# Moving the value projection ahead of the query and key projections, with a pause between those two, in a two-layer cross-attention decoder

## The chip, the core and the metric

The kernel runs on one core of one Trainium2 chip. Its time is device microseconds of one execution. The core has five engines that run side by side, each through its own list of instructions in order: PE (matrix products; "PEld" is its loading of weights), DVE (vector engine), ACT (scalar engine), POOL (a second, slower vector engine) and SP (which issues the transfers here). They wait for each other on semaphores. A product lands in PSUM, a small memory that DVE and ACT read and empty.

## What is computed

Two decoder layers, one after the other, on 16 sequences of 256 positions with 128 features. Each layer has self-attention, cross-attention over 1601 context positions, and a mixture of experts (8 experts with the best 2 chosen; layer two has one shared expert more). Cut to the attention of layer one:

```python
Q = (q_in @ wq + bq).reshape(Bq, Sq, H, HD)      # H = 16 heads of HD = 8
Kp = (k_in @ wk + bk).reshape(Bq, Sk, H, HD)
V = (v_in @ wv + bv).reshape(Bq, Sk, H, HD)
scores = jnp.einsum('bqhd,bkhd->bhqk', Q, Kp) / jnp.sqrt(jnp.float32(HD))
scores = jnp.where(mask, scores, -jnp.inf)       # causal, self-attention only
o = jnp.einsum('bhqk,bkhd->bqhd', jax.nn.softmax(scores, axis=-1), V)
...
x = layernorm(x + attn(x, x, x, ...)); x = layernorm(x + attn(x, enc, enc, ...)); x = layernorm(x + moe(x, ...))
```

Layer two uses root-mean-square norms ahead of each part, masks that are given as integers, and SiLU in its experts.

## The kernel before, in words

**Rounds.** The work of one batch entry in one layer is spread over three rounds. Round t (t = -1 to 32) does the cross-attention of item t, the experts of item t-1 and, in its first 62%, the self-attention, keys and values of item t+1. Items 0 to 15 are layer one, 16 to 31 are layer two. Rounds 2 to 14 are alike (called the layer-one rounds here), and so are rounds 18 to 30 (the layer-two rounds). All engines are restarted between rounds 15 and 16.

**Steps and the planner.** A round is built from steps with two-letter kinds. The lists of steps of one round are merged by a planner (`weave`): each list has a beginning and an end within the round (self-attention 0.03 to 0.62), and a step's place in it goes by the running sum of costs (`COST`) and pauses (`LATER`, and explicit `pause` steps). A pause emits no instruction. It takes a share of its list's stretch, so it moves the steps behind it and squeezes the others together. The merged order is the order of instructions on every engine.

The steps that matter here:

- QP: a projection of queries or keys. PE makes four products 128x256 (L585); DVE adds the bias into the one buffer `q_sum` (L791); POOL makes `q_high` (L1011) and then `qs` (queries), `ks` (keys) or `qc` (cross-attention's queries) from it (L1014). The DVE instruction of a QP waits until POOL is through with the `q_sum` of the QP before.
- SV: self-attention's values. PE makes two products 128x144 (L591), DVE adds the bias (L796).
- KC: keys of the context, in two pieces; PE L732, then two DVE instructions, `k_hi` (L865) and `k_lo` (L867).
- VC: values of the context (L738, L876). 
- MC: maxima of cross-attention's scores, PE L684, DVE L808 in layer one and L815 in layer two. NR (L820) gathers them and NC (L636, L805) writes them into the queries.
- SC, with its mask product L662 in layer two: cross-attention's scores (L670) with the exponential on ACT (L971). WV: their sums with the values (L700).
- MS, SS, NS, WS: the same four kinds for self-attention (L605 and L618 with L801; L612 and L624 with L966; L636 with L805; L645 with L968).
- OT, OPT, OPM: the output projection (L714, L720, L725). XT: a transpose of x (L579), copied on ACT (L964).
- RM1, LN1: norm statistics on DVE. MK: a mask turned from integers to bf16, on DVE (L885), in layer two.
- RT, R2, R3: the router, many short DVE instructions.

**The two rings.** QP, SV, MS, NS, MC, NC, OT, OPM, KC, VC, RT, EBM and ES all take the next of two PSUM tiles, d0 and d1, in turn. PE may start one only when DVE has read the step two places before it in this ring. Another ring of three tiles, a0 to a2, holds SC, SS, WS and the transposes, which ACT reads.

```python
before, size = rings[ring], slots[ring]
x.ring, x.slot = len(before), len(before) % size
x.prior = before[-size] if len(before) >= size else None
```

So a step that is put in or taken out of the d ring changes the tile and the predecessor of every d step behind it.

Of the kernel before, what the change touches and what calls it, by code (L numbers as in the profile page):

```python
# [161 lines left out]
class Plan:  # L162
# [48 lines left out]
    def self_attention(self, l, p):  # L211
        out = []
# [4 lines left out]
        out.append(xt)  # L217
        if not l:
            out.append(self.put("x_in", "RS", "xs x_in", l=l, role="s", p=p))
        out.append(self.put("qs", "QP", "xs", l=l, i=0, p=p))  # L220
        out.append(self.put("ks", "QP", "xs", l=l, i=1, p=p))
        out.append(self.put("vs", "SV", "xs", l=l, p=p))
        out += self.pause(5.0)
        for g in range(NG + 1):
            for pair in (2, 0):
# [1125 lines left out]
```

How the kernel before makes its waits and increments, by code:

```python
    def mark(self, instruction):  # L516
        instruction.then_inc(self.sem, 1)
        self.n += 1
# [21 lines left out]
def wait_made(engine, M, x):  # L540
    if x.kind in D_RING:
        engine.wait_ge(M["d_read"], in_ring(x))
    elif x.kind in A_RING:
        engine.wait_ge(M["a_read"], in_ring(x))
    elif x.kind == "LX":
        engine.wait_ge(M["x_loaded"], 16 * nth(x))
    elif x.kind == "LN2":
        engine.wait_ge(M["ln_scaled"], nth(x))
    elif x.kind == "RM2":
        engine.wait_ge(M["rm_done"], nth(x))
    elif x.kind == "RS":
        engine.wait_ge(M["bias_added"], nth(x))
# [2 lines left out]
def wait_empty(pe, M, x):  # L556
    if x.prior:
        pe.wait_ge(M["d_read" if x.kind in D_RING else "a_read"], in_ring(x.prior))
        if x.prior.kind == "EF" and x.prior.l == 1:
            pe.wait_ge(M["silu_done"], x.prior.j + 1)
    return x.slot
# [2 lines left out]
def tensor_program(pe, T, M, order):  # L565
# [12 lines left out]
            for qt in range(QT):  # L578
                last = pe.transpose(tile[:, qt * P:(qt + 1) * P], source[:, qt, :], T["ident"][:])
            last.then_inc(M["a_made"], 1)
        elif x.kind == "QP":
            source = T["xT_c" if x.i == 2 else "xT_s"]
            pe.wait_ge(M["a_read"], in_ring(x.of["xc" if x.i == 2 else "xs"]))
            for g in range(NG):
                last = pe.matmul(tile[:, g * S:(g + 1) * S], T["w_pad"][:, x.l, x.i, g, :], source[:], start=True,
# [1 line left out]
            last.then_inc(M["d_made"], 1)  # L587
        elif x.kind == "SV":
            pe.wait_ge(M["a_read"], in_ring(x.of["xs"]))
            for kt in range(QT):
```

## Time and profile before

| | us |
|---|---|
| median of three runs | 5493.64 |
| lowest and highest | 5491.49 and 5499.58 |
| the profiled execution | 5490.66 |
| its span, first to last instruction | 5489.3 |
| PE busy | 4937.0 (90%) |
| DVE busy | 3496.5 (64%) |
| ACT busy | 2792.3 (51%) |
| POOL busy | 641.3 (12%) |

Times within the trace are microseconds from the first instruction. A busy time is the union of an engine's instructions. In a row of the timeline, the bracket at the end is the time for which the engine sat idle before it, and the instruction that ended this. The granted clock of PE has two levels, 1.2 GHz (0.5) and 2.4 GHz (1.0); a mean over a stretch lies between.

### The profile page before, as it was taken

What the parts mean: (1) busy time and instruction counts of PE and PEld (TensorE: products, weight loads), DVE (VectorE), ACT (ScalarE), POOL (GpSimd) and SP (SyncE); (2) the same over time, 40 slices, a digit from 0 to 9 for tenths busy, and PEclk for the clock granted to TensorE, in tenths of its full rate; (3) what the DMA queues carried; (4) which work ended last, traced back from release to release, by engine and by line L of the source; (5) the groups of instructions that cost most, each with busy time, mean ns of one, the idle gap of its engine ahead of it and who ended that gap; (6) DMA issues with size and microseconds to landing.
All of it is one profiled execution on the core that took longest, in us unless ns stands there. A gap on an engine that the chain in (4) does not pass through costs nothing.

```text
span 5489.3 us, 101033 instructions
## 1 busy us (share of the span) xinstructions
PE 4937.0 (90%) x40898; PEld 2789.8 (51%) x41312; DVE 3496.5 (64%) x6335; ACT 2792.3 (51%) x5505; POOL 641.3 (12%) x660
## 2 busy tenths in 40 slices
PE   5888888888888888889899999999999999999999
PEld 2455555555555555555355544554455544554456
DVE  4666666665666666665566667666666666666664
ACT  1565565666655555665454444444444444444444
POOL 1111111111111111111110001101010101101000
PEclk7799999999999999998899999999999999999999
DMA  2112222222221222222122222222222222222211
GB/s 59 34 45 54 47 43 47 58 54 57 47 55 44 43 47 58 53 67 66 49 73 73 68 62 73 72 64 75 62 72 72 72 64 67 73 70 68 68 47 64
DMA packets 167976, 326.96 MB, mean 60 GB/s; under 512 B 25656, under 2 KB 76624, under 8 KB 167520
## 3 DMA queue, kind: packets, MB, share of 16 engines
q1 hardware_dynamic: 167520, 320.49, 23.6%
q8 instruction: 334, 5.47, 0.4%
q14 instruction: 122, 1.00, 0.1%
HBM read 237.40 MB, written 4.19 MB: 44 GB/s over the span
## 4 chain that ended last, share of the span: by engine, by line
PE 43%; DVE 4%; ACT 2%; issue 1%; POOL 1%; DVEq 0%
PE a L662 7%; PE sums L700 7%; PE a L670 6%; PE d L776 6%; PE a L764 5%; PE d L684 3%; DVE d L815 2%; ACT probs_c L971 1%; PE d L738 1%; PE d L585 1%; PE a L612 1%; PE d L732 1%; PE a L645 1%; PE d L605 1%; PE d L618 1%
## 5 line engine op out<-in xcount | busy, mean ns | idle before, releaser
L971 ACT ACTIVATE probs_c<-a 128x512 f32<-128x512 f32 (+1 forms) x3584 | 1833.9, 563 | 2084.6 <-PE a L670 2082.7
L815 DVE CUSTOM_DVE_ANT_0 d<-d,mcross_q 128x808 f32<-128x808 f32 x1024 | 1023.3, 1012 | 470.9 <-PE d L684 468.0
L808 DVE TENSOR_REDUCE chunk_max<-d 128x2 f32<-128x808 f32 x1024 | 1003.5, 998 | 288.7 <-PE d L684 280.1
L700 PE MATMUL sums<-probs_c,vc 128*32 128x256 f32 x13312 | 1113.6, 408 | 13.0 <-PEq L1238 12.8
L684 PE MATMUL d<-kc,qc 24*128 24x404 f32 x4096 | 1080.3, 433 | 34.0 <-DVE chunk_max L808 11.1
L670 PE MATMUL a<-qc,kc 25*128 25x256 f32 (+1 forms) x6656 | 934.4, 340 | 130.0 <-ACT probs_c L971 98.9
L670 PEld LDWEIGHTS a<-qc,kc 25*128 25x128 f32 (+1 forms) x6656 | 548.1, 187 | 820.4 <-issue 387.4
L776 PE MATMUL d<-w_back,hidden 128*128 128x128 f32 x4352 | 567.3, 285 | 25.8 <-DVE chunk_max L815 25.8
L776 PEld LDWEIGHTS d<-w_back,hidden 128*128 128x128 f32 x4352 | 542.7, 200 | 73.9 <-DVE chunk_max L815 34.7
L764 PE MATMUL a<-xT_e,w_in 128*128 128x256 f32 x2176 | 579.3, 413 | 0.0
L952 DVE SCALAR_TENSOR_TENSOR xe<-d,comb,xe 128x128 f32<-128x128 f32 x544 | 165.8, 347 | 589.6 <-PE d L776 589.6
L684 PEld LDWEIGHTS d<-kc,qc 24*128 24x128 f32 x4096 | 499.9, 192 | 74.1 <-DVE chunk_max L808 35.0
L662 PE MATMUL a<-mcross_k,ident_b 128*128 128x512 bf16 (+1 forms) x1507 | 482.9, 375 | 59.9 <-ACT probs_c L971 26.7
L764 PEld LDWEIGHTS a<-xT_e,w_in 128*128 128x128 f32 x2176 | 419.3, 203 | 94.9 <-issue 33.7
L700 PEld LDWEIGHTS sums<-probs_c,vc 128*32 128x32 f32 x13312 | 275.3, 111 | 357.9 <-issue 201.7
L966 ACT ACTIVATE probs_s<-a 128x512 f32<-128x512 f32 x512 | 277.9, 594 | 263.6 <-PE a L624 263.6
L801 DVE TENSOR_REDUCE nm_s<-d 128x4 f32<-128x1024 f32 x256 | 313.5, 1225 | 120.8 <-PE d L618 120.7
L662 PEld LDWEIGHTS a<-mcross_k,ident_b 128*128 128x128 bf16 (+1 forms) x1792 | 143.8, 99 | 436.9 <-issue 272.6
L944 DVE SCALAR_TENSOR_TENSOR hidden<-hidden,a 128x512 f32<-128x512 f32 x288 | 198.1, 688 | 126.2 <-ACT hidden L994 125.1
L990 ACT ACTIVATE hidden<-a,b_hid 128x256 f32<-128x256 f32 x512 | 208.6, 476 | 90.6 <-PE a L764 87.1
L1043 POOL TENSOR_TENSOR rstd_s<-mean_var_s,halves 128x2 f32<-128x2 f32 x32 | 22.5, 703 | 1931.4 <-DVE mean_var_s L857 1931.4
L994 ACT ACTIVATE hidden<-a 128x512 f32<-128x512 f32 x288 | 172.0, 597 | 97.9 <-PE a L764 96.3
(157 smaller groups left out, 4358.0 us busy)
## 6 DMA issues: line engine op xcount, KB each, us to landing
w_in<-in_experts SPq DMA_DIRECT2D x272, 256.0 KB, 3.1
w_back<-in_experts SPq DMA_DIRECT2D x272, 256.0 KB, 2.9
kc<-k_hi SPq DMA_DIRECT2D x1024, 50.0 KB
ctxT<-in_ctxT SPq DMA_DIRECT2D x32, 800.5 KB, 5.0
kc<-k_lo SPq DMA_DIRECT2D x512, 50.0 KB
mask_words<-in_mcross SPq DMA_DIRECT2D x32, 800.5 KB
mask_words<-in_mcrossT SPq DMA_DIRECT2D x32, 768.0 KB
out_x<-xe SPq DMA_DIRECT2D x32, 128.0 KB, 1.8
```

Of the source, the lines that this page charges most:

```text
L662: pe.matmul(T["a"][y.slot][0:y.kn, 0:n * S], T["ident_b"][0:y.kn, 0:y.kn], mask, start=True, stop=False)
L670: last = pe.matmul(T["a"][y.slot][0:y.kn, half * S:(half + 1) * S], T["kc"][rows, y.g, kt * P:kt * P + y.kn], T["qc"][y.p][rows, y.g, :], ...
L684: last = pe.matmul(d[:, h * BANK:h * BANK + CHUNK], T["qc"][y.p][rows, y.g, y.i * P:(y.i + 1) * P], T["kc"][rows, y.g, k0:k0 + CHUNK], sta ...
L700: last = pe.matmul(acc[HP * j:HP * j + HP, :], T["vc"][x.p][0:x.kn, v0:v0 + HP], probs_of(T, x)[0:x.kn, j, half:half + S], start=x.j == 0, ...
L764: last = pe.matmul(tile[:, half * S:(half + 1) * S], T["w_in"][load.slot][:, f * P:(f + 1) * P], T["xT_e"][:], start=True, stop=True)
L776: last = pe.matmul(tile[:, qt * D:(qt + 1) * D], hid[:, f, qt * P:(qt + 1) * P], T["w_back"][load.slot][:, f * D:(f + 1) * D], start=f == ...
L801: dve.tensor_reduce(maxima[:, x.j:x.j + 2, :, MROW], tile[:].rearrange("p (h q k) -> p h q k", h=2, q=QT), AX, ALU.max, negate=True).then_ ...
L808: done = dve.tensor_reduce(T["chunk_max"][:, x.g % 2, x.i, x.j:x.j + 2, x.c], tile[:].rearrange("p (h n) -> p h n", h=2)[:, :, 0:CHUNK], A ...
L815: done = dve.tensor_tensor_reduce(both, both, mask, 1.0, -3e38, ALU.add, ALU.max, T["chunk_max"][:, x.g % 2, x.i, x.j, x.c:x.c + 1])
L966: act.activation(T["probs_s"][:, x.j, :], tile[:], ACT.Exp, scale=SCALE).then_inc(M["a_read"], 1)
L971: act.activation(probs_of(T, x)[0:x.kn, x.j, 0:n], tile[0:x.kn, 0:n], ACT.Exp, scale=SCALE).then_inc(M["a_read"], 1)
L990: done = act.activation(T["hidden"][x.i % 2][:, f, :], tile[:, half * S:(half + 1) * S], ACT.Gelu, bias=T["b_hid"][:, x.i, f:f + 1])
```

## The change

Self-attention's values (SV) are put ahead of its queries and keys (QP, twice), and a pause of 3.0 units of the planner stands between the queries and the keys:

```diff
+        out.append(self.put("vs", "SV", "xs", l=l, p=p))
         out.append(self.put("qs", "QP", "xs", l=l, i=0, p=p))
+        out += self.pause(3.0)
         out.append(self.put("ks", "QP", "xs", l=l, i=1, p=p))
-        out.append(self.put("vs", "SV", "xs", l=l, p=p))
         out += self.pause(5.0)
```

No instruction is added or removed. On PE in a layer-one round, before, from the product of the query projection on (`xT_s,w_pad` is QP, `ctxT,w_key` KC, `w_val,xT_s` SV, `kc,qc` into `d` MC, `qc,kc` into `a` SC):

```order
1622 L585 MATMUL d<-xT_s,w_pad 128x256 x4
1623 L732 MATMUL d<-ctxT,w_key 128x512 x2
1624 L700 MATMUL sums<-probs_c,vc 32x256 x4
1625 L670 MATMUL a<-qc,kc 128x256 x2
1626 L684 MATMUL d<-kc,qc 128x404 x2
1627 L670 MATMUL a<-qc,kc 128x256 x2
1628 L585 MATMUL d<-xT_s,w_pad 128x256 x4
1629 L591 MATMUL d<-w_val,xT_s 128x144 x2
```

and after it, from the value projection on:

```order
1617 L592 MATMUL d<-w_val,xT_s 128x144 x2
1618 L715 MATMUL d<-ident,o_c 128x128 x8
1619 L701 MATMUL sums<-probs_c,vc 32x256 x4
...
1624 L586 MATMUL d<-xT_s,w_pad 128x256 x4
1625 L733 MATMUL d<-ctxT,w_key 128x512 x2
1626 L701 MATMUL sums<-probs_c,vc 32x256 x4
1627 L671 MATMUL a<-qc,kc 128x256 x2
1628 L685 MATMUL d<-kc,qc 128x404 x2
...
1634 L721 MATMUL a<-ident,tmp_e 128x128 x2
1635 L586 MATMUL d<-xT_s,w_pad 128x256 x4
```

SV now stands ahead of the previous item's output transposes (OT), and a whole further beat (WV, SC and MC) and a transpose stand between the context keys and the key projection.

On PE in a layer-two round, before (`ident,tmp_e` is a transpose, `w_out,oT_e` the output projection OPM, `mcross_k,ident_b` a mask product):

```order
6553 L585 MATMUL d<-xT_s,w_pad 128x256 x4
6554 L700 MATMUL sums<-probs_c,vc 32x256 x4
6555 L662 MATMUL a<-mcross_k,ident_b 128x512 x2
6556 L670 MATMUL a<-qc,kc 128x256 x2
6557 L684 MATMUL d<-kc,qc 128x404 x2
6558 L670 MATMUL a<-qc,kc 128x256 x2
6559 L591 MATMUL d<-w_val,xT_s 128x144 x2
6560 L725 MATMUL d<-w_out,oT_e 128x128 x2
```

and after:

```order
6561 L726 MATMUL d<-w_out,oT_e 128x128 x2
6562 L701 MATMUL sums<-probs_c,vc 32x256 x4
6563 L663 MATMUL a<-mcross_k,ident_b 128x512 x2
6564 L671 MATMUL a<-qc,kc 128x256 x2
6565 L685 MATMUL d<-kc,qc 128x404 x2
6566 L671 MATMUL a<-qc,kc 128x256 x2
6567 L586 MATMUL d<-xT_s,w_pad 128x256 x4
6568 L733 MATMUL d<-ctxT,w_key 128x512
6569 L733 MATMUL d<-ctxT,w_key 128x65
```

The key projection has moved behind the output projection, next to the second piece of the context keys; SV has gone to a place ahead of the query projection.

On DVE at the same place after the change (`mcross_q<-mask_words` is MK, the `ISA` pair is one MC):

```order
2577 L838 TENSOR_TENSOR xe<-d,mid 128x256
2578 L886 TENSOR_SCALAR mcross_q<-mask_words 128x1601
2579 L816 ISA d,chunk_max<-d,mcross_q 128x2x404
2580 L816 ISA chunk_max 128x1
2581 L792 TENSOR_TENSOR q_sum<-d,b_pad 128x1024
2582 L866 TENSOR_SCALAR k_hi<-d,b_k 128x577
2583 L868 SCALAR_TENSOR_TENSOR k_lo<-d,b_k,k_hi 128x577
```

The key projection's `q_sum` stood ahead of MK before and stands behind it now. The SP list is the same; on POOL one instruction changes place in two rounds. Behind the key projection, MS, SS, NS and WS come a little later against the beats of cross-attention, and with other tiles.

## Rows read from the trace of the kernel before

**Rows 1.** The page, part 1: busy us, share of the span, instructions.

```profile
PE 4937.0 (90%) x40898; PEld 2789.8 (51%) x41312; DVE 3496.5 (64%) x6335; ACT 2792.3 (51%) x5505; POOL 641.3 (12%) x660
```

**Rows 2.** Busy time by stretch: layer-one rounds 4 and 5, layer-two round 22.

```profile
727.00:880.60 153.60, 134.23 (x1225) 80.64 (x1228) 98.82 (x156) 93.74 (x185) 23.16 (x23) 0.94 0.23 52
880.60:1037.70 157.10, 137.86 (x1227) 83.08 (x1232) 98.80 (x156) 93.71 (x185) 23.18 (x23) 0.91 0.22 51
...
3709.10:3886.60 177.50, 167.15 (x1336) 89.56 (x1356) 119.14 (x239) 80.53 (x161) 16.90 (x18) 0.98 0.27 69
```

The columns are: stretch, its length, busy us (and count) of PE, PEld, DVE, ACT, POOL, then the granted clock, the DMA share and GB/s.

**Rows 3.** Who waited for whom, in total: us, times, longest.

```profile
DVE q_sum L791 <- POOL qs L1014: 37.1, 17, 2.9
```

**Rows 4.** Idle time of PE and PEld ahead of QP (L585): us, times.

```profile
  DVE k_lo L867: 50.4, 28
```

**Rows 5.** The same ahead of SV (L591).

```profile
  DVE q_sum L791: 34.9, 30
```

**Rows 6.** Timeline of PE in layer-one round 5, at the key projection.

```profile
898.85 1.99 PE L585 MATMUL d<-xT_s,w_pad 128*128 128x256 f32 x8 [1.70 <-DVE k_lo L867]
900.68 0.65 PE L591 MATMUL d<-w_val,xT_s 128*128 128x144 f32 x4
901.26 0.64 PE L700 MATMUL sums<-probs_c,vc 128*32 128x256 f32 x8
```

**Rows 7.** Timeline of DVE there.

```profile
896.19 1.28 DVE L865 TENSOR_SCALAR k_hi<-d,b_k 128x1024 fp32r<-128x1024 f32 x1 [0.49 <-PE d L732]
897.51 1.28 DVE L867 SCALAR_TENSOR_TENSOR k_lo<-d,b_k,k_hi 128x1024 fp32r<-128x1024 f32 x1
898.71 0.99 DVE L808 TENSOR_REDUCE chunk_max<-d 128x2 f32<-128x808 f32 x1
900.88 1.23 DVE L791 TENSOR_TENSOR q_sum<-d,b_pad 128x1024 f32<-128x1024 f32 x1 [1.18 <-PE d L585]
```

**Rows 8.** Timeline of PE later in round 5, at MS, NS and MS.

```profile
908.89 0.60 PE L605 MATMUL d<-causal_q,ident_b 128*128 128x512 bf16 x2 [0.58 <-DVE chunk_max L808]
...
913.08 0.44 PE L636 MATMUL d<-ident,nm_s 128*128 128x128 f32 x2 [0.77 <-DVE k_lo L867]
...
915.58 0.60 PE L605 MATMUL d<-causal_q,ident_b 128*128 128x512 bf16 x2 [0.60 <-DVE chunk_max L808]
```

**Rows 9.** Timeline of PE in round 5, at the router's second part (R2).

```profile
934.30 0.45 PE L684 MATMUL d<-kc,qc 24*128 24x404 f32 x2 [0.31 <-DVE chunk_max L808]
936.58 0.69 PE L636 MATMUL d<-ident,nm_s 128*128 128x128 f32 x2 [1.83 <-DVE chunk_max L808]
```

**Rows 10.** Timeline of PE in layer-two round 20, at SV and the output projection.

```profile
3377.65 0.76 PE L591 MATMUL d<-w_val,xT_s 128*128 128x144 f32 x4 [1.01 <-DVE q_sum L791]
3378.62 0.96 PE L725 MATMUL d<-w_out,oT_e 128*128 128x128 f32 x4 [0.21 <-DVE chunk_max L815]
```

**Rows 11.** Timeline of DVE there.

```profile
3376.37 1.22 DVE L791 TENSOR_TENSOR q_sum<-d,b_pad 128x1024 f32<-128x1024 f32 x1 [2.23 <-POOL qs L1014]
3377.51 1.00 DVE L815 CUSTOM_DVE_ANT_0 d<-d,mcross_q 128x808 f32<-128x808 f32 x1
3378.42 0.14 DVE L815 DVE_READ_ACCUMULATOR2_ANT chunk_max<- 128x1 f32 x1
3378.44 0.46 DVE L796 TENSOR_TENSOR vs<-d,b_val 128x288 f32<-128x288 f32 x1
3379.62 0.42 DVE L837 TENSOR_TENSOR xe<-d,mid 128x256 f32<-128x256 f32 x1 [0.72 <-PE d L725]
3379.96 2.14 DVE L885 TENSOR_SCALAR mcross_q<-mask_words 128x1601 bf16<-128x1601 int32 x1
...
3384.62 0.82 DVE L867 SCALAR_TENSOR_TENSOR k_lo<-d,b_k,k_hi 128x577 fp32r<-128x577 f32 x1
```

**Rows 12.** Busy time by stretch, in stretches of half clock; columns as Rows 2.

```profile
883.80:894.00 10.20, 8.24 (x39) 5.73 (x40) 4.73 (x7) 2.70 (x6) 0.39 (x1) 0.50 0.63 152
...
934.90:941.90 7.00, 5.32 (x44) 2.23 (x46) 3.83 (x12) 1.67 (x4) 0.00 (x0) 0.51 0.01 2
...
3379.00:3382.40 3.40, 3.40 (x19) 1.12 (x18) 2.48 (x2) 0.00 (x0) 2.25 (x1) 0.51 0.03 7
```

## The prediction

> **What bounds the kernel now.** I read the shares of busy time first. PE is busy for 90% of the span and DVE for 64% [rows 1], so the end is set by PE, and a change of order can only gain where PE idles or runs slowly. 5489.3 - 4937.0 leaves 552 us of idle PE. Then I read busy time by round. The layer-one rounds take 157.1 us, but rounds 4 and 6 take 153.6 with the same work: same counts and the same DVE time, but 3.6 us less of PE time, at a granted clock of 0.94 in place of 0.91 [rows 2]. So a round has two costs that the order can move: waits, and stretches in which the clock is granted at 1.2 instead of 2.4 GHz. Layer-two rounds take 177.5 us at a clock of 0.98 with PE busy for 167 us: some 10 us of idle, close to its floor.
>
> Third, the two places of the change. In layer one the key projection waits 1.70 us for `k_lo` of the context keys [rows 6]: these hold their tile until two DVE instructions of 1.28 us each are done [rows 7], with only one beat of PE between. Ahead of the projections this wait stands 28 times, 50.4 us [rows 4]; each is booked once on PE and once on its weight loads, so it is 14 rounds and half the time. In layer two the context keys come earlier, and another chain is last: the key projection's `q_sum` waits 2.23 us on DVE for POOL to finish the queries [rows 11], 37.1 us in 17 places [rows 3]. Behind it in DVE's list stand the maxima and SV's bias; SV on PE needs the key projection's tile, so it waits 1.01 us, and the output projection 0.21 more [rows 10]; ahead of SV this is 34.9 us in 30 entries, so again 15 rounds [rows 5]. Right after, the clock drops to half for 3.4 us with PE wholly busy [rows 12]. That costs half of 3.4, 1.7 us.
>
> **The change, layer one, per round.** No instruction comes or goes; every term is a wait that goes, moves or appears.
> - SV goes ahead of OT. It takes the tile whose maxima are just being made, the one for which OT waited before, so this wait only changes owner; OT then finds its tile read. SV's own products, 0.65 us, move and are not added: zero. It needs the ACT copy of x, which a beat with two maxima covers; if that cover fails it is some tenths.
> - Between the context keys and the key projection there are now two beats, a transpose and one more d step. DVE needs 1.28 + 1.28 after the keys' product, and then 0.99 for the maxima whose tile the key projection takes [rows 7]. PE's work in the meantime is about 0.6 + 0.4 to the second maxima (they take over the wait for `k_lo`: two sums at 0.57, one beat at 0.5 and 0.3, about 2.0 against 2.9 with the release, so 0.9), then 0.6 up to the key projection (0.99 + 0.1 against 0.6, so 0.5). The 1.70 becomes 1.4: -0.3. So the wait here mostly moves, since DVE is the one that is behind. This is the term that the diff suggests to be the largest, and it is small.
> - The first MS pair stood right behind maxima and waited 0.58; now the second piece of context keys and a beat stand between (over 1.5 us of PE work): -0.6.
> - NS waited 0.77 and the next MS 0.60 [rows 8]. Now NS stands a beat later, behind NC: DVE has two MS reads and a maximum, about 3.8 with the release, PE 2.9: 0.9 in place of 1.37, -0.4 to -0.5.
> - At R2 PE waits 0.31 and 1.83 [rows 9], since NS follows two maxima that queue behind the router's short instructions. NS moves behind one more beat, so the next maxima take the wait, 0.9 of it covered by the sums and the scores; but the maxima of the pair before now take a tile of MS and wait about 0.5. 2.14 becomes 1.5: -0.6.
> - Sum of the waits: -1.9, with bounds -3.7 (all of those listed but the `k_lo` one go) and +0.5.
> - Clock: the stretch at half clock of 7.0 us right behind the 1.83 wait has PE busy for 5.32 us [rows 12], so it is worth up to 2.7 us; the one of 10.2 us starts ahead of everything that is moved and I leave it. I take a bit under half of 2.7, 1.1.
> - Together -3.0, which makes a round of about 154, near the 153.6 that rounds 4 and 6 have already. 13 rounds by -3.0 is -39.
>
> **Layer two, per round.**
> - The wait for POOL goes: there are now some 8 us of PE work between queries and keys, against 1.12 + 2.35 of POOL's and the 1.2 of `q_sum`. PE's 1.01 + 0.21 [rows 10] go: -1.2. DVE's wait of 2.23 [rows 11] goes too.
> - New: the query projection takes the tile of the maxima made right ahead of SV; SV and a transpose cover 1.0 of about 1.5: +0.5.
> - New: the context keys' second piece takes the tile of maxima that stand behind the mask conversion. On DVE from the output projection on: 0.42 + 2.14 + 1.00 + 0.14, 3.7 and 0.3 for the release; on PE the sums, a beat and the key projection, 0.6 + 1.1 + 1.9, 3.6: +0.4. The key projection's `q_sum` was ahead of that conversion before.
> - New: NC came behind both MS before; it is now ahead of them and waits for the gathered maxima. DVE has 0.82 twice for the keys, the norm's statistics (about 0.7), 1.14 and 0.2; PE about 3.4 of work against these 3.7 and the backlog: +0.5. The MS behind it waits for one more maximum, 1.14 less NC's 0.4: +0.7. Some 0.3 of short waits at the old MS pair go.
> - Sum of the waits: +0.6; bounds -1.5 and +0.9.
> - Clock: the half-clock stretch stood right behind the wait that goes [rows 10, 12]. If it goes, -1.7. The new waits are four of 0.4 to 0.7, spread over 17 us.
> - Together -1.1. Over the 15 rounds from 16 on, -17. Rounds 0, 1 and 15 have parts of both: I take -1.3 each, -4.
>
> Sum: -39 - 17 - 4 = -60 us. The profiled execution took 5490.66, 1.4 more than its span and 3.0 under the median; -60 on that is 5431, and on the median of 5493.64 it is 5434. A difference of 0.2%, 11 us, is about what a measurement of this kernel can tell from none.
>
> A rule that speaks against the change: the Trainium skill, page "TensorE: Matmul & The Clock Gate", section "A second HAM failure mode: psum-queue depth-cycling", says that a kernel that cycles PSUM tiles and idles briefly between groups of matmuls can have its clock fall and rise again and pay for that between bursts, with no single long gap. Cutting one wait into two, as in layer one, would then gain no clock. In this trace half-clock stretches do stand behind waits of 1.0 to 1.8 us, which agrees as far as it goes; whether four waits of half a microsecond suffice no row shows.
>
> **The rivals.**
> - *DVE is the local bound and nothing is gained.* For: it has the same instructions, and at the change in layer one its reads queue back to back. Against: DVE itself idles 2.23 us in layer two and 1.18 in layer one at this place [rows 7, 11]. The clock stretches stay too. Then -1.9 is about -0.5 and layer two +0.6: 13 by -0.5 and 15 by +0.6 is +3, 5496.
> - *Slower: short waits keep the clock down in layer two.* Place: from the mask conversion to the first MS. If the waits of +0.9 (upper bound) fall close together, the half-clock stretch stays and a second one of 3.4 us joins it: 0.9 + 1.7 is +2.6 per round, 15 rounds +39, 5533, with layer one unchanged. It decides from the point where two of the new waits, more than about 1.0 us together, fall within a few microseconds, as the 1.01 and 0.21 do now. This is also what the page's rule would give.
> - *Both layers lose one more stretch.* For: rounds 4 and 6 show that a layer-one round can jump by 3.5 us at once, with the same work. If layer two jumps likewise from 177.5 to about 174.1 (both its 3.4 us half-clock stretches gone), it is 28 rounds by -3.4, -95: 5398.
> - *The pause does nothing.* In layer one DVE has no wait for POOL in the regular rounds, so the pause only spaces; but the order shows that the steps move in all rounds, so this has no chance of its own.
>
> **How the numbers follow.** Forecast 0.50 (5434, from -20 to -80); both layers jump 0.14 (5398); no change 0.15 (5496); slower 0.21 (5533). Faster is 0.50 + 0.14 = 0.64, same 0.15, slower 0.21. The range reaches from 5390, under the double jump, to 5535, just over the price of the slower rival; what is left out is a slower case worse than priced and a faster one with more than both stretches, somewhat under 0.2. The forecast's own range is 5414 to 5474.
>
> **What would show it.** Right: the key projection's wait for `k_lo` in layer one under 1 us, no wait of DVE for POOL, no SV wait in layer two, layer-one rounds at 153 to 155 us and a clock of 0.93 or more, layer-two rounds at 174 to 177. Wrong: layer-two rounds at 178 or more with waits of PE ahead of the context keys, NC and MS; layer-one rounds still at 157 with a new half-clock stretch. The weakest term is the clock: it carries over half of the forecast, and rests on stretches that follow waits, not on a wait that I can sum. The restart in the middle and the rounds around it may also shift by some microseconds either way.

## The result, and the profile of the changed kernel

| | before | after |
|---|---|---|
| median, us | 5492.57 | 5637.99 |
| lowest and highest | 5483.88 to 5499.58 | 5624.65 to 5642.89 |
| the profiled execution | 5490.66 | 5634.89 |
| its span | 5489.3 | 5633.6 |
| mean granted clock | 0.936 | 0.913 |

Four runs of each. The ratio is 1.0255, with a 95% interval of 1.0227 to 1.0283: slower by 145 us. I had forecast 5434 and a range up to 5535. The sign is wrong, and the time lies 103 us above the range.

Lines of the changed kernel are one higher than before from the change on: QP is L586, SV L592, the two maxima L809 and L816, RM1 L858, MK L886. The first part of its page, which answers to [rows 1]:

```profile
PE 5140.4 (91%) x41312; PEld 2839.9 (50%) x41312; DVE 3503.8 (62%) x6335; ACT 2797.7 (50%) x5505; POOL 640.1 (11%) x660
```

DVE, ACT and POOL have the same work in the same time. Only PE has 203 us more. Some of that is bookkeeping: the trace of before lacks 414 matmul records, that of after none. The rest is slower products. The missing ones are mask products (21 per layer-two round, 5 per layer-one round), and where one is missing the row shows idle time. Busy time by stretch, first the 13 layer-one rounds 2 to 14, then the 13 layer-two rounds 18 to 30 (columns as [rows 2]; counts that fall short of the other trace's are missing records), of before:

```profile
412.96:2447.29 2034.33, 1783.62 (x15876) 1074.24 (x15939) 1284.60 (x2018) 1217.98 (x2393) 301.31 (x299) 0.92 0.22 51
2999.01:5306.52 2307.51, 2172.89 (x17356) 1170.43 (x17628) 1547.32 (x3105) 1047.34 (x2081) 219.65 (x234) 0.98 0.27 69
```

and of after:

```profile
414.32:2485.97 2071.65, 1832.76 (x15941) 1082.87 (x15939) 1285.67 (x2018) 1223.41 (x2393) 300.79 (x299) 0.91 0.22 50
3030.76:5450.77 2420.01, 2315.11 (x17629) 1211.85 (x17629) 1556.05 (x3105) 1047.88 (x2081) 219.28 (x234) 0.94 0.25 65
...
3402.80:3590.30 187.50, 179.48 (x1357) 93.86 (x1357) 119.82 (x239) 80.57 (x161) 16.87 (x18) 0.93 0.25 66
3434.40:3458.30 23.90, 22.80 (x108) 8.88 (x109) 12.24 (x20) 5.92 (x13) 1.72 (x4) 0.50 0.20 27
```

Layer one lost 37 us, 2.9 per round; layer two lost 112.5, 8.7 per round; all the rest of the program gained 5.5. That is where the 144 us between the two spans went. Length less PE's busy time gives the idle time of a round, 18.4 us in layer one and 8.1 in layer two. The rows of before would give 19.3 and 10.4, but they count the missing products as idle. Two kernels of the experiments have the order of before in one of the layers, rounds as long, as much time at half clock, and complete records. Rounds 2 to 14 of the one (values first in layer two only) and rounds 18 to 30 of the other (added products in layer one only):

```profile
415.36:2449.64 2034.28, 1793.41 (x15941) 1074.30 (x15939) 1284.02 (x2018) 1217.98 (x2393) 301.26 (x299) 0.92 0.22 51
2951.45:5258.79 2307.34, 2217.01 (x17629) 1168.27 (x17628) 1547.25 (x3105) 1047.35 (x2081) 219.61 (x234) 0.98 0.26 69
```

They give 18.5 and 6.9 us. So idle time is no part of the loss in layer one, and 1.1 us of the 8.7 in layer two. The clock is the rest: layer-two rounds now take 187.5 and 184.5 us by turns, and have a stretch of 23.9 us (seven rounds, the last row) or 17.1 us (six rounds) at half clock, where before one of 6.8 or two of 3.4 us stood ([rows 12] has the first of the two in round 20).

**What happens in layer two.** Round 20 of after starts at 3402.80. The forecast's gains came: in this round SV and the output projection wait for nothing, and over the whole trace DVE's wait for POOL ahead of `q_sum` is down from 37.1 us in 17 places [rows 3] to one place of 0.7. Then, on DVE:

```profile
3425.67 1.12 DVE L886 TENSOR_SCALAR mcross_q<-mask_words 128x1601 bf16<-128x1601 int32 x1
...
3430.64 0.82 DVE L868 SCALAR_TENSOR_TENSOR k_lo<-d,b_k,k_hi 128x577 fp32r<-128x577 f32 x1
3431.37 2.31 DVE L858 CUSTOM_DVE_ANT_0 tmp_e<-xe 128x128 f32<-128x128 f32 x1
3433.62 0.08 DVE L858 DVE_READ_ACCUMULATOR2_ANT mean_var_e<- 128x1 f32 x1
3433.62 0.28 DVE L858 CUSTOM_DVE_ANT_0 tmp_e<-xe 128x128 f32<-128x128 f32 x1
3433.83 0.08 DVE L858 DVE_READ_ACCUMULATOR2_ANT mean_var_e<- 128x1 f32 x1
3433.83 1.00 DVE L816 CUSTOM_DVE_ANT_0 d<-d,mcross_q 128x808 f32<-128x808 f32 x1
3434.75 0.14 DVE L816 DVE_READ_ACCUMULATOR2_ANT chunk_max<- 128x1 f32 x1
3434.92 0.17 DVE L821 TENSOR_REDUCE nm_c<-chunk_max 128x8 f32<-128x16 f32 x1
```

on POOL:

```profile
3431.18 2.35 POOL L1015 TENSOR_TENSOR ks<-q_sum,q_high 128x1024 fp32r<-128x1024 f32 x1
```

and on PE:

```profile
3435.24 0.66 PE L637 MATMUL d<-ident,nm_c 128*128 128x128 f32 x2 [2.25 <-DVE nm_c L821]
3436.16 1.04 PE L606 MATMUL d<-mself_q,ident_b 128*128 128x512 bf16 x2 [0.26 <-DVE chunk_max L816]
...
3456.89 2.40 PE L739 MATMUL d<-w_val,ctxT 128*128 128x144 f32 x12
...
3642.23 1.74 PE L739 MATMUL d<-w_val,ctxT 128*128 128x144 f32 x12
```

RM1, the sum of squares of a 128x128 tile, is two instructions of 0.28 us. The first of them takes 2.31 us here and ends 0.15 us after POOL's `ks`, which began 0.19 us ahead of it. Both read two inputs from SBUF, the memory in which the engines keep their tiles. The maxima and their gathering queue behind it, so NC on PE waits 2.25 us. The clock falls within that wait and stays at half for 23.9 us in which PE is busy for 22.8. What PE does there is short of large products in f32: scores and maxima with 24 or 25 rows, sums of 32 columns, masks in bf16 and a few transposes. Here it rises 1.4 us after the context's values (L739, twelve full-size records) have begun. But in the rounds with 17.1 us it rises among the small ones, 3.0 us ahead of them: round 21's stretch ends at 3639.2. Who waited for whom in total (us, times, longest), and then the form of RM1 over the whole trace (min, median and max ns):

```profile
PE d L637 <- DVE nm_c L821: 34.1, 20, 2.2
```

```profile
L858 DVE CUSTOM_DVE_ANT_0 tmp_e<-xe x32: 279/289/2315, 2874.9 to 5591.6; 128x128 f32<-128x128 f32 x32
```

The same form has 280/286/293 ns before. The Trainium skill, page "SBUF — State Buffer", section "Who interferes with whom", says that a DVE instruction with two SBUF inputs contends with a GpSimd instruction that reads SBUF, and that the port pair they share is an exclusive lock; this trace agrees, 2.31 us for 0.28.

**What happens in layer one.** Round 5 of after starts at 892.00. On PE:

```profile
909.15 0.45 PE L685 MATMUL d<-kc,qc 24*128 24x404 f32 x2 [0.54 <-DVE k_lo L868]
913.37 0.71 PE L726 MATMUL d<-w_out,oT_e 128*128 128x128 f32 x4 [0.32 <-DVE q_sum L792]
...
919.55 0.61 PE L606 MATMUL d<-causal_q,ident_b 128*128 128x512 bf16 x2 [0.97 <-DVE k_lo L868]
923.13 0.44 PE L637 MATMUL d<-ident,nm_c 128*128 128x128 f32 x2 [0.58 <-DVE nm_s L802]
924.04 0.44 PE L637 MATMUL d<-ident,nm_s 128*128 128x128 f32 x2 [0.47 <-DVE chunk_max L809]
```

and three of its half-clock stretches:

```profile
925.60:929.00 3.40, 3.40 (x24) 1.12 (x22) 1.93 (x2) 2.02 (x4) 0.00 (x0) 0.50 0.01 2
942.70:946.10 3.40, 3.40 (x22) 1.25 (x22) 1.76 (x2) 1.14 (x3) 0.00 (x0) 0.50 0.00 0
949.50:956.30 6.80, 6.78 (x47) 2.54 (x47) 3.75 (x11) 2.29 (x6) 0.00 (x0) 0.50 0.00 0
```

The key projection's wait of 1.70 [rows 6] is gone, and 0.54 + 0.32 stand in its place. But the round takes 161.2 us, for two reasons. There are new stretches of 3.4 us, the first of them at 925.60, behind three waits of 0.97, 0.58 and 0.47; the one of 10.2 us at the round's beginning is down to 3.4. And the half-clock time moved off the waits: before, the stretches of 10.2 and 7.0 us had PE busy for only 8.24 and 5.32 [rows 12], so part of the slow time fell where PE stood anyway. Summed over rounds 2 to 14, 3.4 us per round of half-clock time coincided with idle PE before and 0.45 after. By this reckoning, which no experiment tests by itself, a wait that goes from under such a stretch gives back half of its length only.

### The profile page after: what moved, and what is told of

The parts are those of the page before. It is cut to its first block, busy times and chain, and to the rows that moved or that the text cites. A ratio compares the mean times of both kernels' runs of the same rounds, so it can differ in the third digit from the quotient of the medians.

```text
span 5633.6 us, 101461 instructions
## 1 busy us (share of the span) xinstructions
PE 5140.4 (91%) x41312; PEld 2839.9 (50%) x41312; DVE 3503.8 (62%) x6335; ACT 2797.7 (50%) x5505; POOL 640.1 (11%) x660
## 4 chain that ended last, share of the span: by engine, by line
PE 45%; DVE 5%; SPq 1%; issue 1%; ACT 1%; DMA 0%; POOL 0%; DVEq 0%
PE sums L701 8%; PE a L663 7%; PE d L777 6%; PE a L671 5%; PE a L765 5%; PE d L685 4%; DVE d L816 2%; PE d L606 2%; PE d L586 2%; PE a L613 1%; PE d L619 1%; PE d L739 1%; PE a L646 1%; SPq L1077 1%; DVE tmp_e L858 1%
## 5 line engine op out<-in xcount | busy, mean ns | idle before, releaser
L816 DVE CUSTOM_DVE_ANT_0 d<-d,mcross_q 128x808 f32<-128x808 f32 x1024 | 1023.3, 1011 | 569.9 <-PE d L685 568.9
L809 DVE TENSOR_REDUCE chunk_max<-d 128x2 f32<-128x808 f32 x1024 | 1001.0, 997 | 272.6 <-PE d L685 264.3
L701 PE MATMUL sums<-probs_c,vc 128*32 128x256 f32 x13312 | 1139.2, 416 | 12.9 <-PEq L1239 12.7
L685 PE MATMUL d<-kc,qc 24*128 24x404 f32 x4096 | 1100.8, 439 | 51.5 <-DVE chunk_max L809 13.3
L671 PE MATMUL a<-qc,kc 25*128 25x256 f32 (+1 forms) x6656 | 950.2, 344 | 126.3 <-ACT probs_c L972 100.8
L663 PE MATMUL a<-mcross_k,ident_b 128*128 128x512 bf16 (+1 forms) x1792 | 551.0, 383 | 13.5 <-ACT probs_c L972 13.4
L685 PEld LDWEIGHTS d<-kc,qc 24*128 24x128 f32 x4096 | 511.3, 195 | 93.2 <-DVE chunk_max L809 34.3
```

Of the source, the lines that this page charges most:

```text
L663: pe.matmul(T["a"][y.slot][0:y.kn, 0:n * S], T["ident_b"][0:y.kn, 0:y.kn], mask, start=True, stop=False)
L671: last = pe.matmul(T["a"][y.slot][0:y.kn, half * S:(half + 1) * S], T["kc"][rows, y.g, kt * P:kt * P + y.kn], T["qc"][y.p][rows, y.g, :], ...
L685: last = pe.matmul(d[:, h * BANK:h * BANK + CHUNK], T["qc"][y.p][rows, y.g, y.i * P:(y.i + 1) * P], T["kc"][rows, y.g, k0:k0 + CHUNK], sta ...
L701: last = pe.matmul(acc[HP * j:HP * j + HP, :], T["vc"][x.p][0:x.kn, v0:v0 + HP], probs_of(T, x)[0:x.kn, j, half:half + S], start=x.j == 0, ...
L809: done = dve.tensor_reduce(T["chunk_max"][:, x.g % 2, x.i, x.j:x.j + 2, x.c], tile[:].rearrange("p (h n) -> p h n", h=2)[:, :, 0:CHUNK], A ...
L816: done = dve.tensor_tensor_reduce(both, both, mask, 1.0, -3e38, ALU.add, ALU.max, T["chunk_max"][:, x.g % 2, x.i, x.j, x.c:x.c + 1])
```

## The experiments

Each time is the median of the runs, with the ratio to the kernel before run on the same chip (medians of before 5493.64, 5501.92, 5493.82 and 5502.63). Stretch rows have the columns of [rows 2]; two long rows are rounds 2 to 14 and 18 to 30 of that kernel, as above.

### Each half alone

Values first, no pause (the change without its pause line):

```diff
         out.append(self.put("qs", "QP", "xs", l=l, i=0, p=p))
-        out += self.pause(3.0)
         out.append(self.put("ks", "QP", "xs", l=l, i=1, p=p))
```

> The changed kernel without the pause: values ahead of queries and keys, and nothing else. Theory (the pause does the harm in layer two, by pushing the key projection behind the mask conversion and next to the context keys, so that POOL's work on the keys, 2.35 us, falls on the norm's statistics): without it the statistics are not stalled, PE has no wait of 2 us ahead of NC, no half-clock stretch over 7 us in the layer-two rounds, and these take 174 to 178 us; in all about 5480 to 5530. Rival (the moved values do the harm by turning the tiles of the ring over): layer-two rounds stay at 184 to 188 us and the time at about 5620.

Measured 5492.1 us, 0.9995 [0.9978, 1.0012].

The pause alone, in the kernel before:

```diff
         out.append(self.put("qs", "QP", "xs", l=l, i=0, p=p))
+        out += self.pause(3.0)
```

> The kernel before with the pause of 3.0 between queries and keys, values still behind the keys. Theory (the pause does the harm): layer-two rounds of 182 us or more with a half-clock stretch of over 10 us, 5580 to 5650. Rival (the moved values do it): within 0.5% of the kernel before, 5465 to 5520.

Measured 5537.5 us, 1.0083 [1.0057, 1.0109], between the times of my theory and of the rival: both were wrong. Rounds 2 to 14 and 18 to 30, of the pause alone:

```profile
409.24:2494.94 2085.70, 1835.53 (x15875) 1089.35 (x15939) 1284.47 (x2018) 1223.52 (x2393) 300.74 (x299) 0.89 0.22 50
3032.40:5346.45 2314.05, 2176.74 (x17356) 1183.52 (x17628) 1529.17 (x3105) 1048.56 (x2081) 219.12 (x234) 0.99 0.27 68
```

and of the values first alone, layer two:

```profile
3010.42:5303.82 2293.40, 2158.17 (x17356) 1167.93 (x17628) 1529.01 (x3105) 1047.95 (x2081) 228.94 (x234) 0.99 0.27 69
```

The pause costs layer one 4.0 us per round by itself (160.4 against 156.5), nothing much in layer two (178.0). The values first gain 1.1 per round in layer two (176.4) and cost 0.8 in layer one (157.3). So the layer-one loss is the pause's, and the 8.7 per layer-two round belong to neither: they come only when both are there, which is where RM1 meets `ks`. With either half alone no RM1 of the experts' input takes over 0.3 us.

The values first do not save the wait either. It goes over to the output projection, here in a kernel that has them first in layer two only (further below):

```profile
3369.86 0.71 PE L728 MATMUL d<-w_out,oT_e 128*128 128x128 f32 x4 [1.02 <-DVE q_sum L794]
```

SV's 1.01 and the output projection's 0.21 have become 1.02 for the output projection; the 1.1 us per round come from the half-clock time, which is down from 6.8 to 4.2 us.

### Taking the collision away

The change, with RM1 of the experts' input moved behind the gathered maxima and the next pair of maxima:

```diff
+        if x.kind == "RM1" and x.role == "e":
+            ...
+                k = rest.index("MC", rest.index("NR", n))
+                ...
+                    order.insert(k, order.pop(n))
```

> The changed kernel, with one DVE step moved in the layer-two rounds: the norm's statistics of the experts' input (RM1, line 858) stand behind the gathering of the maxima and the next maxima, not ahead of them. Theory (they are stalled by 2 us by POOL's product for the keys, the maxima queue behind them, NC waits 2.2 us, and this wait lets the clock fall for 17 to 24 us): the statistics take 0.3 us again, NC's wait is under 0.5 us, the long half-clock stretch is gone and layer-two rounds take 172 to 177 us; the time is 5634 less about 13 rounds by 9, so 5500 to 5530. Rival (the clock falls there whatever the wait, since the new order puts all thin products together): the wait goes, and the half-clock stretch stays at over 13 us; rounds of 182 to 186 us, about 5600.

Measured 5514.48 us, 1.0037 [1.0015, 1.006]. NC waits for nothing and only the MS behind it for 0.79 (PE, and rounds 18 to 30):

```profile
3409.76 0.44 PE L654 MATMUL d<-ident,nm_c 128*128 128x128 f32 x2
3410.99 0.60 PE L623 MATMUL d<-mself_q,ident_b 128*128 128x512 bf16 x2 [0.79 <-DVE chunk_max L833]
```

```profile
3023.37:5337.45 2314.08, 2186.53 (x17356) 1183.96 (x17628) 1529.11 (x3105) 1048.42 (x2081) 219.98 (x234) 0.98 0.27 68
```

186.2 us per layer-two round is 178.0 now, with all other instructions where the change puts them. This gives back 8.1 of the 8.7. I had 172 to 177: in six of the 13 rounds a stretch of 6.8 or 10.2 us now stands at 48 to 50 us of the round, and what starts it is not known.

The change, with POOL's `ks` made for one of four groups of heads in layer two (it leaves out the keys of the other three):

```diff
-            pool.tensor_tensor(dest[:], T["q_sum"][:], T["q_high"][:].bitcast(F32),
+            n = 1 if x.i == 1 and x.l == 1 else NG
+            pool.tensor_tensor(dest[:, 0:n, :], T["q_sum"][:, 0:n, :], T["q_high"][:, 0:n, :].bitcast(F32),
```

> The changed kernel, where POOL's second product for self-attention's keys in layer two is made on the first of the four groups only (a quarter of the columns; the keys of the other three are left out, so the output is not the reference's). Theory (the statistics of the experts' input, RM1 on line 858, take 2.31 us in place of 0.28 because POOL's product of 2.35 us on SBUF runs at that time, and that wait leads to NC's and to the half clock): with about 0.6 us of POOL work the statistics take under 0.7 us, NC waits under 0.8 us and the half-clock stretch of 17 to 24 us at 31.6 us of the round is gone or under 7 us; the time is 5500 to 5560, as with the statistics moved. Rival (the place in DVE's list matters and not POOL): statistics still 2.3 us and the stretch stays, 5620 to 5640.

Measured 5566.19 us in one run. RM1 stays in place, and takes 0.69 us beside a POOL instruction of 0.74 us that began 0.20 ahead of it (DVE, PE, and a stretch):

```profile
3426.10 0.69 DVE L858 CUSTOM_DVE_ANT_0 tmp_e<-xe 128x128 f32<-128x128 f32 x1
```

```profile
3428.34 0.41 PE L637 MATMUL d<-ident,nm_c 128*128 128x128 f32 x2 [0.62 <-DVE nm_c L821]
3429.27 0.60 PE L606 MATMUL d<-mself_q,ident_b 128*128 128x512 bf16 x2 [0.52 <-DVE chunk_max L816]
```

```profile
3430.40:3444.10 13.70, 13.37 (x73) 4.77 (x66) 6.79 (x10) 3.26 (x8) 0.00 (x0) 0.50 0.11 11
```

RM1's time follows POOL's, which settles the collision. The clock is not settled so simply: behind waits of 0.62 and 0.52, the same in all 13 rounds, it still falls in two, for 13.7 us in round 20, while round 22 has only 3.4 in all and takes 176.5. In six others a stretch of 10.2 us stands at 48.7 us of the round. On the mean a round takes 179.6. What makes the difference between one round and the next is not shown.

### Making the same delay without the pause

The values first without the pause, and six small DVE products, each waiting for the one before, ahead of RM1:

```diff
+            if x.role == "e":
+                for n in range(6):
+                    ln.mark(dve.tensor_tensor(tmp[:, 0, :], value[:, 0, :], value[:, 0, :], ALU.mult))
+                    dve.wait_ge(ln.sem, ln.n)
```

> Self-attention's values first and no pause (5492.1, layer-two rounds of 176.4 us), and six additional products of 128x128 values on DVE ahead of the statistics of the experts' input in layer two, each waiting for the one before: some 0.28 us and a short wait each, about 2 us in all, the size of the stall that POOL causes in the changed kernel. My theory: it is the late maxima and the wait of PE behind them that let the clock fall, not the pause and not POOL's work as such. Then PE waits about 1 to 2 us here too, ahead of the first step that needs these maxima, a longer half-clock stretch stands behind it, and layer-two rounds take 180 to 187 us: 5545 to 5650. The rival: the long half-clock stretch comes from the order of steps that the pause makes in this place (thin products close together), and a wait alone gives only itself: layer-two rounds of 177 to 178.5 us, 5500 to 5525. Nothing: the delay is covered on DVE, PE doesn't wait, and 5492 stays.

Measured 5632.11 us, 1.0224 [1.018, 1.0269]. On DVE and PE, then round 20 and its two long stretches at half clock:

```profile
3417.46 1.91 DVE L858 TENSOR_TENSOR tmp_e<-xe 128x128 f32<-128x128 f32 x6
```

```profile
3420.96 1.01 PE L605 MATMUL d<-mself_q,ident_b 128*128 128x512 bf16 x2 [1.78 <-DVE chunk_max L815]
```

```profile
3387.70:3577.00 189.30, 180.88 (x1357) 92.89 (x1356) 119.71 (x245) 80.64 (x161) 17.57 (x18) 0.92 0.25 65
3421.00:3434.70 13.70, 13.70 (x67) 4.73 (x68) 7.30 (x12) 2.69 (x6) 1.24 (x3) 0.50 0.00 0
3451.80:3465.50 13.70, 13.70 (x79) 4.17 (x75) 6.29 (x18) 4.82 (x10) 0.00 (x0) 0.50 0.00 0
```

1.91 us of DVE work per round, on an engine that is busy for two thirds of it, made the program 140 us slower than the same kernel without it (5492.1; 131 if the 9 us are taken off by which the kernel before, too, was slower beside it): 9.4 us per layer-two round for a wait of 1.78. PE is busy for every bit of both stretches. The first begins as the wait of 1.78 ends, the second 1.5 us after the end of a wait of 1.01. They end 4.4 and 5.0 us ahead of the next large products, among small ones. The delay, by whatever it is made, is enough; pause and POOL were only its makers in the change.

### Full-size products behind the wait

The change, with six products 128x128x256, whose result nobody reads, behind the second NC of layer two; then four of them behind that NC of layer one instead (`x.l == 0`, `range(4)`):

```diff
+            if x.kind == "NC" and x.l == 1 and x.g == 1:
+                for n in range(6):
+                    last = pe.matmul(tile[:, BANK:BANK + S], T["w_key"][:, 1, :], ...)
```

> The changed kernel with work added: six products of a full 128x128 weight with 256 columns behind the first NC of each layer-two round, into an unused part of its tile, result not used. At half clock they take 6 by 0.8, 4.8 us, at full clock 2.3 us. Theory (the clock does not rise again there because the products that follow have 24 or 25 rows or 32 columns, and it rises with full ones): the half-clock stretch ends within a few us behind them, 7 to 10 us long in place of 17 to 24, and the rounds get shorter although work was added: 180 to 184 in place of 184.5 to 187.5, 5570 to 5610 in all. Rival (what is in the products does not matter): the stretch keeps its 17 to 24 us and the rounds get longer by 2.3 to 4.8 us, 5670 to 5700.

Measured 5602.33 us, 1.0186 [1.0147, 1.0225]. PE's wait is the same, the stretch at half clock short (PE; the stretch; rounds 18 to 30):

```profile
3431.23 0.66 PE L637 MATMUL d<-ident,nm_c 128*128 128x128 f32 x2 [2.24 <-DVE nm_c L825]
3431.68 3.99 PE L640 MATMUL d<-w_pad,w_key 128*128 128x256 f32 x12
```

```profile
3430.80:3434.20 3.40, 2.97 (x8) 2.48 (x9) 1.26 (x5) 0.00 (x0) 1.41 (x3) 0.50 0.00 0
...
3033.88:5401.49 2367.61, 2222.01 (x17513) 1223.52 (x17785) 1556.51 (x3105) 1047.90 (x2081) 219.29 (x234) 0.98 0.26 67
```

With 4 us of work added (3.98 to 5.33 from round to round), a round is 4 us shorter: 182.1 for 186.2, and the stretch is 3.4 or 6.8 us long (in one round of the 13 none comes). So the wait starts the stretch, and what PE does next has a part in how long it lasts. Which property of the products counts, their size, their type or their place, no run separates.

> The changed kernel with four full 128x128 by 256 columns products added behind the first NC of each layer-one round (at about 32 us of it), 1.6 us at full clock, result not used. Theory (thin products let the clock fall there): the half-clock stretch at 33.5 us of the round goes, and with some luck the next one; rounds of 157 to 161 us with about the same or a shorter time than the changed kernel's 160.3 although 1.6 us of work was added, 5610 to 5645 in all. Rival (kind of product does not matter in layer one, only the waits): the stretch stays where it is and rounds take 162 to 164, 5660 to 5690.

Measured 5627.25 us, 1.0237 [1.0219, 1.0254]. Some 1.9 us of products more, and layer-one rounds are 159.1 for 159.4, which is no difference: in three other kernels with the layer-one order of the change they take 160.1. The new stretch at 33.5 us into the round is gone in most of them and pays for the products, no more.

### Other places of the kernel

The context's values begin and end earlier (0.15 to 0.51 of the round in place of 0.2 to 0.6), on the values first without the pause:

```diff
-        side += [(0.02, 0.2, plan.keys(l, p)), (0.2, 0.6, plan.values(l, p)),
+        side += [(0.02, 0.2, plan.keys(l, p)), (0.15, 0.51, plan.values(l, p)),
```

> Values first without a pause, and the context values (VC, twelve full products a time) spread over 0.15 to 0.51 of the round in place of 0.20 to 0.60, so that the first ones stand at about 33 us of a layer-one round and the second at about 52, where the half-clock stretches of the run with values first alone begin (34.0 and 54.5). Theory (the clock falls and stays down where thin products stand together, and full ones hold it up): these two stretches go or shrink, layer-one rounds take 150 to 154 us in place of 157.0, and the time is 5430 to 5470. Rival (they fall where PE waits for DVE, whatever the products): the stretches stay or move, rounds of 157 or more and a time within 0.3% of the 5492 of values first, or above.

Measured 5553.31 us, 1.0105 [1.0076, 1.0134]. Layer two stayed at 176.3, but layer one rose from 157.3 to 163.0 per round. The first half-clock stretch there grew from 6.8 to 10.2 us and others moved. My theory, that full-size products in the right places hold the clock up, had 150 to 154 us, and is wrong here; the rival, that the clock falls where PE waits, had 157 or more. What made it 6 us is open.

Values first in layer two only, no pause:

```diff
+        if l:
+            out.append(self.put("vs", "SV", "xs", l=l, p=p))
```

> The kernel before, with the values ahead of queries and keys in layer two only, and no pause. The traces so far: with values first in both layers the regular layer-two rounds took 176.4 us on the mean in place of 177.5, the layer-one rounds 157.3 in place of 156.5. If layers are separate: 156.5 and 176.4, so 13 by -1.1, about 14 us less, 5475 to 5485 (-0.1% to -0.3%). Rival (the rounds fall in and out of patterns by what came before, so that such means don't carry over): within 0.2% of before either way.

Measured 5472.58 us, 0.9963 [0.9947, 0.9979], with rounds of 176.5 us in layer two, some at 174.6 and a clock of 1.00:

```profile
3345.30:3519.90 174.60, 167.69 (x1361) 88.71 (x1360) 117.68 (x239) 80.63 (x161) 17.61 (x18) 1.00 0.27 70
```

The kernel before, with three unread products 128x128x256 ahead of the transpose of x in layer one, behind which PE waited 0.88 us for ACT; then, as well, three of 108 columns behind one pair of maxima:

```diff
+            if x.role == "s" and x.l == 0:
+                for n in range(3):
+                    pe.matmul(tile[:, S:2 * S], T["w_key"][:, 1, :], ...)
```

> The kernel before with work added in layer one: three full 128x128 by 256 products, 1.2 us at full clock, ahead of self-attention's transpose (at 2.3 us of the round), result not used. PE waits 0.86 and 0.67 us right behind it in the kernel before, and the half-clock stretch of 10.2 us begins at 3.2. Theory (half clock comes where waits and thin products leave the array with little to do, and full products in place of a wait hold it up): the stretch at 3.2 goes in most rounds, and rounds take 153.5 like rounds 4 and 6 of the kernel before; 5445 to 5465. Rival (the waits are only pushed back and the clock falls all the same): rounds of 157 to 160.5, 5495 to 5545.

Measured 5460.23 us, 0.9937 [0.9913, 0.9962].

> As with the full products ahead of the transpose, and three more of 108 columns behind the maxima that stand ahead of the 1.83 us wait at the router (about 53.7 us of a layer-one round), where the half-clock stretch of 6.8 us begins at 54.4. Theory: that stretch goes too; rounds of 150 to 153.5, 5400 to 5460. Rival (added products only add or move things): no shorter than with the first three alone, 5470 to 5560.

Measured 5444.58 us, 0.9916 [0.989, 0.9942]. On PE and for rounds 2 to 14 of the first of the two:

```profile
893.84 1.56 PE L580 MATMUL a<-w_pad,w_key 128*128 128x256 f32 x6
```

```profile
427.67:2427.58 1999.91, 1772.68 (x16018) 1063.46 (x16016) 1284.25 (x2018) 1219.30 (x2393) 301.26 (x299) 0.94 0.22 52
```

1.56 us of useless work per round, which also fills that wait of 0.88, makes the round 2.7 us shorter (153.8 for 156.5), since the stretch of 10.2 us is gone. All layer-one rounds but the first of them are now what rounds 4 and 6 were before. The second addition kept 153.6, but the next stretch, of 6.8 us, stayed where it was; I had expected it to go.

The first of the two shows something else in layer two, where nothing was changed. Its last three regular rounds take 180.9, 180.9 and 188.4 us, and have stretches at half clock of 10.2 and, in the last, 13.7 us (round 30):

```profile
5105.00:5293.40 188.40, 180.98 (x1359) 93.52 (x1359) 118.49 (x237) 80.68 (x161) 16.92 (x18) 0.92 0.23 57
```

Waits of 0.5 and 0.18 us stand ahead of the first stretch in each of the three, with no RM1 held up. So a wait of 2 us is enough for a long stretch, but not needed for one, and the order of before can fall into it too.

Both additions together, with the values first in layer two only:

> The kernel before with two things that each helped alone: the full-size products in layer one of the run before (they brought layer-one rounds from 156.5 to 153.6 us, 5444.6 in all), and self-attention's values ahead of its queries in layer two only, without the pause (layer-two rounds from 177.5 to 176.5 us, 5472.6 in all). The two act in different rounds, so both theories that see a round as a thing of its own expect the sum: 5492.6 - 48 - 20 = about 5425, with layer-one rounds of 153.6 and layer-two rounds of 176.5. If the length of a round depends instead on where in its clock's rhythm the round before ended, the gains don't add: 5440 to 5460.

Measured 5444.81 us, 0.99 [0.9861, 0.9939]: the fastest together with the run of both additions, not faster (0.99 against 0.9916, with intervals that overlap). Rounds 2 to 14 and 18 to 30:

```profile
417.75:2414.63 1996.88, 1790.07 (x16096) 1079.71 (x16095) 1285.22 (x2018) 1218.54 (x2393) 300.53 (x299) 0.94 0.23 52
2954.31:5249.06 2294.75, 2204.07 (x17630) 1169.39 (x17629) 1529.01 (x3105) 1047.78 (x2081) 228.52 (x234) 0.99 0.27 69
```

Within these rounds the gains do add: 37.5 and 12.8 us. My sum of 5425 had counted more than that, since each kernel alone had also gained around the restart of the engines (rounds 15 to 17 took 545 us in one, 542 in the other, against 552), and 540 together; rounds -1 to 1 took 388 against 386 and 383; and round 31, 133.6 us in each, is 142.1 here.

## Why the prediction was wrong

**Right: most of the waits.** Layer two: SV's 1.01 and the output projection's 0.21 went, and so did DVE's 2.23 for POOL. The query projection's new wait, put at 0.5, and that of the context keys, put at 0.4, do not show in round 20, and the MS behind NC waits 0.26, not 0.7. Layer one: the 1.70 became 0.54 + 0.32, where I had 1.4, for the reason given, that the second maxima take over the wait for `k_lo`. The NS pair has 0.47 and 0.58 for 0.77 and 0.60. I had the first MS pair lose its 0.58; it has 0.97, since the second piece of the context keys, which I had put ahead of it as cover, brings its own `k_lo`. At the router 0.83 and 0.46 stand in place of 0.31 and 1.83 (I had 1.5 for the two together), and 0.54 ahead of its own product is new. Together the idle time of a layer-one round fell by 0.2, not 1.9 (my bounds were -3.7 to +0.5; the waits that I listed for the first add up to 4.1), and that of a layer-two round rose by 1.1, where I had +0.6 and at most +0.9. Both are reckoned against the complete records of the result section; the 10 us of idle that I read in a layer-two round of before were 7 us and missing records.

**Wrong: the wait of NC, priced at +0.5.** I took about 0.7 for the statistics on DVE, and from the first of them to the maxima it took 2.5 (3431.37 to 3433.83), which made a wait of 2.25: my 0.5 and the 1.8 by which that term was too low. The trace of before had the collision in its rows, one step up: MK with its 2.14 us [rows 11] is slow only beside POOL (the same instruction of 128x1601 takes 0.99 where POOL is idle, and 2.07 to 2.69 beside it). I used that 2.14 as MK's price, expected the context keys to wait 0.4 behind it, and did not ask why it was twice what its size asks. After the change MK takes 1.12, the keys wait for nothing, and the stall has gone over to RM1, which stands where it hurts. The step that failed is the term "the norm's statistics (about 0.7)" in the wait of NC: I priced RM1 by what it takes when POOL is idle, and MK by what it takes beside POOL. In these two the duration belongs to the place, not to the instruction.

**Wrong: the sign of the clock terms, -1.1 and -1.7 per round.** The stretch that stood behind SV's wait did go, as forecast. I gave the new waits no stretch of their own, since they were to be four of 0.4 to 0.7, spread over 17 us. A new one came behind the single wait of 2.25, of 17.1 or 23.9 us. Half-clock time per layer-two round rose from 6.8 to 24.2 us, and the part of it that coincides with idle PE from 0.2 to 1.3 (means over the 13 rounds): (17.3 - 1.1) / 2 is 8.1, and 1.1 of idle time make 9.2. Measured are 8.7. In layer one it rose from 25.7 to 30.2, and the part of it that coincides with idle PE fell from 3.4 to 0.45: (4.5 + 2.95) / 2 = 3.7, less 0.2 of idle time, is 3.5, where 2.9 were measured. So the reckoning has the right size and is half a microsecond too high in both layers, for which I have no row.

**The rival that came.** The slower one had the right place (from the mask conversion to the first MS) and the right mechanism (waits behind which the clock falls). The point from which it was to decide (over about 1.0 us together) is not settled: a wait of 0.79 alone started nothing in this place, 0.62 and 0.52 did so in two rounds of 13, 1.78 in all 13; in the kernel with products added in layer one 0.49 and 0.18 stood ahead of no stretch in two rounds and ahead of 10.2 us in three others. Its price was 2.6 us per round, since I let the new stretch be as long as the old one of round 20, 3.4 us (in seven of the 13 rounds that one is 6.8 long). Behind NC come 20 us of small products, and behind SV's wait the output projection and the context keys. That this makes the difference fits the products added behind NC; but in round 20 of before the clock was up again at 3382.4, just when the context keys began, and above it rose among small products too, so it is not shown. The price was too low by the factor in length, and the range, which ended at that price, too narrow. The rival also had layer one unchanged, while the pause alone costs it 4.0 per round.

That rival had the rule of the Trainium skill in it (page "TensorE: Matmul & The Clock Gate", section "A second HAM failure mode: psum-queue depth-cycling"), by which short idle times between groups of products make the clock fall and rise, and the cost is paid between bursts. The trace agrees as to the short waits: one of 1.78 us was enough. It goes further than that rule, in that the clock stayed low for 13.7 us with PE busy throughout.

**What stays open.** Why layer-one rounds with the pause settle at 160.4 us and those of the earlier context values at 163.8, with no or 1 us more idle time than at 157.0. Most layer-one rounds of all kernels have one of four lengths, 3.4 us apart (153.6, 157.0, 160.4, 163.8), as long as the shortest stretch at half clock seen; it may be that a small shift costs either a step or nothing. Layer-two rounds don't keep to such steps (174.5, 176.1, 177.5 and 178.9 in one kernel). No experiment tells which of the small waits tips it, so the cause of the layer-one loss, a quarter of the whole, is open.

## What to carry to other kernels

Where a trace shows stretches at half clock, do not price a moved or new wait by its length alone: behind SV's wait stood 3.4 or 6.8 us at half clock, and behind NC's, ahead of a long run of small products, 17.1 or 23.9. Before using a duration from the trace for an instruction that moves, look whether another engine's work lies beside it there and will lie beside it in its new place; a vector instruction at twice the time of its equals is a sign. Before comparing the idle time of two traces, compare the counts of their products: here 21 missing records per round looked like 3.4 us of waiting. And ask of each moved step what it now runs beside, not only what it now waits for.

## What the hardware did that was not expected

- PE stays at half clock for 13.7 us with no idle time in it at all (13.70 busy of 13.70), and for up to 23.9 us with 1.1 us idle. In these stretches most products had 24 or 25 rows or 32 columns, or were masks in bf16. It rose 1.4 us into full-size products in the stretches of 23.9 us, but 3.0 us ahead of them in those of 17.1.
- Adding products made rounds shorter twice: 1.56 us ahead of a transpose gave 2.7 us (0.88 of the added time filled a wait), 4 us behind NC gave 4. A third addition, 1.9 us in layer one of the change, gave nothing.
- A DVE instruction can be held until POOL's is through: 0.28 us became 2.31 beside a POOL instruction of 2.35, and 0.69 beside one of 0.74.
- A wait under a half-clock stretch seems to cost only half, since half-clock time in which PE stands does no slow work: reckoned so, the two layers lose 9.2 and 3.5 us per round, where 8.7 and 2.9 were measured.
